# Recurrent attention in a two-layer kernel: another order of the same operations on four engines

## The reference

```python
Fcum = jnp.cumsum(logfg, axis=-1)
Dmat = Fcum[..., :, None] - Fcum[..., None, :] + i_pre[..., None, :]
Dmat = jnp.where(causal, Dmat, -jnp.inf)
m = jnp.max(Dmat, axis=-1, keepdims=True)
Smat = jnp.exp(Dmat - m)
qk = jnp.einsum('bhsd,bhtd->bhst', q, k) / jnp.sqrt(jnp.float32(dqk))
C = qk * Smat
n = jnp.maximum(jnp.abs(jnp.sum(C, axis=-1, keepdims=True)), jnp.exp(-m))
h = jnp.einsum('bhst,bhtd->bhsd', C / n, v)
...
h_out = jax.nn.sigmoid(o_pre) * h_norm
x1 = x + h_out @ w_out
```

## Time and profile before

| | us |
|---|---|
| median of 3 runs (lowest, highest) | 697.85 (697.79, 698.93) |
| the profiled execution's own time | 698.43 |
| its span in the trace | 696.5 |
| PE busy, share of the span | 669.8, 96% |
| DVE | 517.4, 74% |
| ACT | 372.0, 53% |
| POOL | 131.1, 19% |

### The profile page before, as it was taken

The page is one execution under the profiler, slowest core; times in us unless marked ns, Lnnn a source line. Parts: engine busy times, 40 slices in busy tenths (PEclk is TensorE's granted clock), DMA queues, the critical chain, the costliest instruction groups (busy, mean ns, idle before and its releaser), DMA issues.

```text
span 696.5 us, 12153 instructions
## 1 busy us (share of the span) xinstructions
PE 669.8 (96%) x4808; PEld 560.3 (80%) x4808; DVE 517.4 (74%) x919; ACT 372.0 (53%) x775; POOL 131.1 (19%) x125
## 2 busy tenths in 40 slices
PE   7998998999999999999999999999999999999996
PEld 7866775778787888878888878887777898889886
DVE  6736778887956576566675575757679998989996
ACT  5886878846644444344353442446666455364541
POOL 7144535410000020000200002000123213203220
PEclk9999999999999999999999999999999999999999
DMA  5099452000101001010001100150000000000000
GB/s 196 5 264 299 105 155 71 2 1 0 63 1 31 0 1 63 0 31 1 1 23 40 32 1 0 42 233 2 0 1 0 1 2 31 1 31 1 1 31 31
DMA packets 24008, 31.27 MB, mean 45 GB/s; under 512 B 1232, under 2 KB 19952, under 8 KB 23184
## 3 DMA queue, kind: packets, MB, share of 16 engines
q1 hardware_dynamic: 23296, 29.18, 13.6%
q10 hardware_dynamic: 656, 1.31, 0.5%
HBM read 28.18 MB, written 2.31 MB: 44 GB/s over the span
## 4 chain that ended last, share of the span: by engine, by line
PE 66%; DVE 23%; ACT 6%; issue 3%; POOL 1%; DMA 1%; DVEq 0%
PE bank L94 21%; PE bank L96 19%; PE bank L95 19%; DVE l_ring_lo L2544 3%; DVE l_ge L2525 2%; DVE l_h L2540 2%; DVE l_o L2548 1%; DVE h_raw L1220 1%; DVE l_h L2497 1%; ACT m_W L709 1%; PE bank L519 1%; DVE h_ring_lo L1225 1%; DVE m_st L938 1%; PE bank L507 1%; PE bank L492 1%
## 5 line engine op out<-in xcount | busy, mean ns | idle before, releaser
L1220 DVE TENSOR_TENSOR h_raw<-h_s,bank 128x512 f32<-128x512 f32 x104 | 71.4, 686 | 107.9 <-ACT h_s L1210 93.5
L1210 ACT ACTIVATE h_s<-bank 128x512 f32<-128x512 f32 x104 | 62.2, 598 | 164.1 <-PE bank L96 164.0
L1225 DVE TENSOR_TENSOR h_ring_lo<-h_raw,h_ring_hi 128x512 fp32r<-128x512 f32 x92 | 68.9, 749 | 0.1
L1214 ACT ACTIVATE h_ring_hi<-h_raw 128x512 fp32r<-128x512 f32 x104 | 64.7, 622 | 2.3 <-DVE h_raw L1220 2.3
L95 PE MATMUL bank<-fused_lo,h_ring_hi 128*128 128x256 f32 x208 | 58.4, 281 | 0.0
L2244 ACT ACTIVATE l_s<-bank 128x512 f32<-128x512 f32 x32 | 19.1, 598 | 62.7 <-PE bank L96 62.5
L94 PE MATMUL bank<-l_xT_hi,l_wgu 128*128 128x512 f32 x128 | 51.2, 400 | 0.3
L94 PE MATMUL bank<-f_yT_hi,mlp_hi 128*128 128x512 f32 x128 | 50.6, 396 | 0.2 <-DVE f_yT_lo L1333 0.2
L96 PE MATMUL bank<-l_xT_hi,l_lo 128*128 128x512 f32 x128 | 50.0, 391 | 0.0
L95 PE MATMUL bank<-l_xT_lo,l_wgu 128*128 128x512 f32 x128 | 50.0, 390 | 0.0
L96 PE MATMUL bank<-f_yT_hi,fused_lo 128*128 128x512 f32 x128 | 50.0, 390 | 0.0
(11 more groups left out here) (372 smaller groups left out, 1972.8 us busy)
## 6 DMA issues: line engine op xcount, KB each, us to landing
m_W<-m_scratch SPq DMA_DIRECT2D x16, 512.0 KB, 6.8
fused_raw<-in_fused SPq DMA_DIRECT2D x1, 3584.0 KB, 12.9
res<-in_x SPq DMA_DIRECT2D x4, 512.0 KB, 6.1
fused_raw<-in_fused SPq DMA_DIRECT2D x2, 1024.0 KB, 9.3
f_mask<-expert_weights SPq DMA_DIRECT2D x8, 256.0 KB
l_raw<-in_layer SPq DMA_DIRECT2D x1, 2048.0 KB, 8.7
out_x<-res SPq DMA_DIRECT2D x16, 128.0 KB, 1.9
f_xw<-in_turned_x SPq DMA_DIRECT2D x3, 512.0 KB, 5.5
```

The source lines that it names most:

```text
L1210: self.nc.scalar.activation(self.s[u % 2][r, :], gate[r, :], ACT.Silu).then_inc(self.silu.sem, 1)
L1214: self.nc.scalar.activation(self.unit(i, u)[0], self.product(i, u), ACT.Copy).then_inc(self.hi.sem, 1)
L1220: self.nc.vector.tensor_tensor(out=self.product(i, u), in0=self.s[u % 2][r, :], in1=up[r, :], op=ALU.mult).then_inc(self.hidden.sem, 1)
L1225: self.nc.vector.tensor_tensor(out=lo, in0=self.product(i, u), in1=f32(hi), op=ALU.subtract).then_inc(self.lo.sem, 1)
```

## The change

The same instructions are issued, in another order on PE, ACT, DVE and POOL; SP's list is the same. The helper `gated_sum` is dissolved into `sum_squares` and `gate`. On PE, in a batch, `score` and `weighted` come earlier against the projections and `local_state`. On ACT `weights(n+4)` comes before the tanh, `high_h` before `copy_values`, `evict(b, 3)` before `weights(n+5)`; at the end two splits come before the last evictions and the silu before `normal_x`. On DVE `normal_x` moves from the end of a batch to between `sum_squares` and `gate`, ahead of the batch's third `weigh_scores`; `weigh_q` goes behind `weigh_scores`. On POOL `after_norm(b-1, 1)` goes from ahead of the masks to behind the last one.

```diff
@@ tensor, start @@
-        following.hid.credit_down(pe)
...
         idle_products(6)
+        following.hid.credit_down(pe)
@@ tensor, batches @@
+            score(n + 1)
             if b:
                 project_k(b + 1)
+            if b:
                 project_q(b + 1)
-            score(n + 1)
             turn_k(b + 1)
+            weighted(b, 0)
+            score(n + 2)
             local_state(b, 0)
-            weighted(b, 0)
             project_v(b + 1, 0)
             if b:
                 turn_h(b - 1, 1)
-            score(n + 2)
             local_state(b, 1)
             weighted(b, 1)
             project_v(b + 1, 1)
+            score(n + 3)
             if b:
                 project_out(b - 1, 1)
             output_gate(b + 1, 0)
-            score(n + 3)
+            weighted(b, 2)
             local_state(b, 2)
-            weighted(b, 2)
             output_gate(b + 1, 1)
             turn_h(b, 0)
+            weighted(b, 3)
             score(n + 4)
-            weighted(b, 3)
             project_out(b, 0)
         b, n = B - 1, N - C
+        weighted(b, 0)
         score(n + 1)
         local_state(b, 0)
-        weighted(b, 0)
         score(n + 2)
         local_state(b, 1)
         weighted(b, 1)
         score(n + 3)
-        local_state(b, 2)
         turn_h(b - 1, 1)
         weighted(b, 2)
+        local_state(b, 2)
@@ scalar, start @@
         copy_k(0)
+        copy_values(0, 0)
         act.wait_ge(const_ready, CONSTANTS)
         copy_q(0)
-        copy_values(0, 0)
         copy_values(0, 1)
-        copy_keys(0)
         act.wait_ge(rows_t, 1)
         nc.scalar.activation(x_rows[0:B * C, 0, :], rows_banks[0], ACT.Copy)
+        copy_keys(0)
...
+        decay_of_queries(0)
         act.wait_ge(dve_tables, DEC)
         nc.scalar.activation(dexp[:, :, :], dec[:, :, :], ACT.Exp).then_inc(act_tables, 1)
-        decay_of_queries(0)
...
         weights(0)
-        decay_of_queries(3)
         copy_k(1)
         weights(1)
+        decay_of_queries(3)
@@ scalar, batches @@
             evict(b, 0)
-            copy_values(b + 1, 0)
             if b:
                 high_h(b - 1, 1)
+            copy_values(b + 1, 0)
             weights(n + 3)
             evict(b, 1)
             copy_values(b + 1, 1)
+            weights(n + 4)
             output_gate(b + 1, 0)
-            weights(n + 4)
             evict(b, 2)
             output_gate(b + 1, 1)
             high_h(b, 0)
+            evict(b, 3)
             weights(n + 5)
-            evict(b, 3)
@@ scalar, end @@
         following.squares(act)
         high_h(b - 1, 1)
+        following.split_high(act, 0, 2)
         evict(b, 2)
         following.scale_y(act)
-        following.split_high(act, 0, 2)
         following.high_y(act)
         evict(b, 3)
         high_h(b, 0)
+        following.silu(act, 0)
         normal_x(b)
-        following.silu(act, 0)
         high_h(b, 1)
         high_h(b, 2)
+        following.hid.act_hi(act, 0, 0)
         following.split_high(act, 2, following.OPEN)
-        following.hid.act_hi(act, 0, 0)
@@ gpsimd, batches @@
                 inverse_root(b - 1, 1)
-                after_norm(b - 1, 1)
             mask_weights(n + 4)
...
             mask_weights(n + 7)
+            if b:
+                after_norm(b - 1, 1)
@@ vector, start @@
-        following.hid.credit_hidden(dve)
...
         low_y(0)
+        following.hid.credit_hidden(dve)
...
+        weigh_scores(0)
         dve.wait_ge(act_tables, EA_K)
         weigh_q(0)
-        weigh_scores(0)
@@ vector, batches @@
                 mean_square(b - 1, 1)
+            if b:
+                sum_squares(b - 1, 1)
+            if b:
                 add(b - 1, 0)
-                gated_sum(b - 1, 1)
+            if b:
+                gate(b - 1, 1)
+            weigh_scores(n + 1)
             weigh_q(b + 1)
-            weigh_scores(n + 1)
...
             mean_square(b, 0)
+            sum_squares(b, 0)
+            normal_x(b)
+            gate(b, 0)
             if b:
                 add(b - 1, 1)
-            gated_sum(b, 0)
...
             weigh_scores(n + 4)
-            normal_x(b)
@@ vector, last batch @@
         mean_square(b - 1, 1)
+        sum_squares(b - 1, 1)
         add(b - 1, 0)
         weigh_scores(n + 1)
         carry(b, 0)
-        gated_sum(b - 1, 1)
+        gate(b - 1, 1)
...
         mean_square(b, 1)
-        gated_sum(b, 1)
+        gate(b, 1)
         following.split_low(dve, 0, 1)
+        sum_squares(b, 1)
         norm(b, 0)
         following.low_y(dve)
         mean_square(b, 2)
-        gated_sum(b, 2)
+        sum_squares(b, 2)
         low_h(b, 0)
+        add(b - 1, 1)
+        gate(b, 2)
+        following.split_low(dve, 1, 2)
         norm(b, 1)
-        add(b - 1, 1)
         norm(b, 2)
-        following.split_low(dve, 1, 2)
         following.hidden(dve, 0)
         low_h(b, 1)
+        add(b, 0)
         low_h(b, 2)
-        add(b, 0)
         following.split_low(dve, 2, following.OPEN)
         add(b, 1)
+        following.split_low(dve, following.OPEN, following.known["mlp_down"])
         add(b, 2)
         following.hid.dve_lo(dve, 0, 0)
-        following.split_low(dve, following.OPEN, following.known["mlp_down"])
```

More of the change, by code:

```diff
@@ L1000, in mean_square @@
             nc.vector.tensor_reduce(out=den[f][3][:, x], in_=sq[:, some, :].rearrange("p c (h d) -> p (c h) d", d=DV), op=ALU.add, axis=AX.X).then_inc(ms_steps.sem, 1)
-        def gated_sum(b, f):
-            sum_squares(b, f)
-            gate(b, f)
         def sum_squares(b, f):
```

## The result

The changed kernel takes 693.09 us (median of 4 runs, 692.77 to 694.83) against 698.16 for the kernel before beside it: ratio 0.9928, 95% interval 0.9914 to 0.9942, so 5.1 us or 0.7% faster. Predicted were 694.0, that is 3.9 us faster. The profiled execution took 692.77 us with a span of 690.9 (before 698.43 and 696.5).

A forecast was written before the change was run, and what follows sets the result against it. TensorE, busy 96% of the span, was taken as the bound, with 9.35 us removable in stalls and slow clock. Batches 2.5, tail 1.3 and last steps 0.1 gave 3.9 us off the median 697.85: 694.0, range 692.4 to 696.9.

The forecast's parts named there:

- batches: Batches before the tail: stalls of 4.11 us become 1.35; less 0.25 for rounding, a gain of 2.5 us.
- Tail: Last batch's attention: stalls of 3.84 us become 3.4 and the slow clock costs less, gain 0.4 + 0.9 = 1.3 us.
- Stalls before project_q, 1.33 and 0.68: project_q waits for add(b-1,0); with normal_x moved and score(n+1) earlier, 0.68 goes and 0.35 of 1.33 is left.
- score(2) ahead of project_v, score(3) ahead of output_gate: Batch 0: scores move into the stalls of 1.06 and 1.04 us; left about 0.3 and 0.4, plus 0.3 before weighted(0,1).
- No new stall inside a batch: TensorE's waits within a batch: margins thin, smallest 0.25 us, counted 0; bound 0.3 us at three places in two batches.
- The masks: GpSimd: masks start earlier without gain; norm may meet them and end 0.4 or 1.5 us late; counted 0.
- The slow clock costs some 0.5 instead of 1.4: Tail: project_out(2,1) at low clock fits into the time before turn_y, which gives 0.9 us of the gain.
- what is late next is ACT: 15 us in a row: Tail, from evict(2,3): ACT's chain of weights, evictions, squares, high_h, splits and scale_y leaves TensorE waits of 1.9 and 0.9 us.
- The low level left as soon as TensorE was busy again.: Argument against a slower result by the clock in the tail, based on the low clock in the earlier profile.
- The tail gives nothing: Rival: ACT's 15 us chain bounds the tail, only the batches gain 2.5 us, 695.35; chance 0.12.
- Slower: the clock: Rival: low clock holds from the tail's idle 1.9 and 0.9 us through gates(1), costing 9 us, 703; chance 0.04.
- Everything fits better: Rival: a third of the stalls left in tail and batches goes and the clock stays high, 2.1 us more, 691.85; chance 0.08.

The follow-up runs named there:

- e2: Kernel before with only the last batch in the new order on all engines, start and loop old: 696.19 us, ratio 0.9959.
- e1: Kernel before with only the loop over batches 0 to 2 in the new order on all four engines: 694.88 us, ratio 0.994.
- e7: Kernel before plus 9 unused 128x128 identity products on TensorE in the last batch's stall of 1.93 us: 698.04 us, ratio 0.9992.
- e4: Changed kernel with normal_x back at the end of the batch on VectorE, behind the fourth weigh_scores: 697.76 us, ratio 0.9985 to the kernel before.
- e11: Kernel before with one edit, normal_x(b) on VectorE moved between sum_squares(b,0) and gate(b,0): 696.48 us, ratio 0.9973.
- e5: Changed kernel with TensorE's old order in the loop; ACT, VectorE and GpSimd keep the new one: 693.81 us.
- e3: Changed kernel with GpSimd's wait after_norm(b-1,1) back ahead of the two masks: 694.66 us.
- e8: Changed kernel with the two weight splits on ACT back behind scale_y: 692.91 us.
- e10: Kernel of e9 plus 7 unused identity products on TensorE ahead of output_gate(0,0), near 30.5 us: 696.68 us.
- e9: Changed kernel with the last batch in another new order (high_h before squares, weighted(3,3) before turn_y, gates before the last project_outs): 695.95 us.
- e12: The changed kernel measured again without any edit, on the chip of e9 to e11: 693.64 us, ratio 0.9931 to the kernel before.

## Why the prediction was right, point by point

- **The sum, 3.9 us.** Measured 5.1 by the medians, 4.5 at equal clock. The terms, from the table: batches 2.5 predicted; measured 0.4 before project_out(0,0) (62.18 in e2, which has the old code and full clock there, against 61.80) and 1.9 in the loop, together 2.3. That these agree is partly luck. The prediction's own figures give 1.1 for batch 0 (1.06 + 1.04 less 0.3 + 0.3 + 0.4) and 1.7 for the two stalls of the loop, before the 0.25 that it takes off; batch 0 gave 0.4 and the loop 1.9. In batch 0 it left out the stall before score(1), 1.08 in e2, which the profile of before hides behind a low clock and which the new order does not remove. Tail 1.3 predicted, 2.3 measured (19.47 to 17.14). Last steps 0.1 predicted, 0.5 measured (566.9 to 566.4); 0.4 of it is the wait for h_ring_lo behind the span's 142 us, 0.71 instead of 1.08 (e1 and e7, with the old tail, have 1.08 and 1.07).
- **Stalls before project_q, 1.33 and 0.68.** Right: predicted 0.35 and none, measured 0.27 and none. The figure of 1.33 itself varies in the old order, 1.33, 1.23 and 0.73 in before, e2 and e7; in the seven other profiles with all the new lists of the loop the wait is under 0.15. That normal_x is the main cause is shown by e4 and e11; that score(n+1) ahead of project_k has a part is shown by e5, where the first stall is 0.83.
- **score(2) ahead of project_v, score(3) ahead of output_gate.** They happen as worked out (score(2) at 46.82, predicted 46.6), and the stalls left at 50.47 and 54.33 are 0.41 and 0.37. But their worth was over-rated: e5 loses 0.2 to 0.7 us in all without them, since the waiting moved to 44.01 and 45.96.
- **No new stall inside a batch.** Right, but for one of 0.15 us before project_v(3,1), one of the two places named as thinnest (0.25 us).
- **The masks.** The step was right: norm is 0.4 to 0.8 us longer, and off TensorE's path, since with norm back at 0.68 (e3) the second batch of the loop takes 22.49 us for 22.51. The Trainium skill's rule (SBUF — State Buffer, Who interferes with whom) agrees with norm at 69.47 and 91.98 and with L1002 at 63.08, 1.12 us instead of 0.19. It does not hold for the pow, which also reads SBUF: L1025 at 119.15 took 0.68 us beside it.
- **The tail: the term that was mis-sized.** "The slow clock costs some 0.5 instead of 1.4" counted time that was no loss: e7 takes the slow clock away and gains 0.4, because ACT and VectorE set the end. And "what is late next is ACT: 15 us in a row" (its terms add up to 14.5) named one of two bounds; by e8 it is VectorE's list that holds gates(0). The stalls came out near: 0.6, 1.9 and 0.9 predicted, 0.70, 1.63 and 0.71 measured. The gain came from where I saw it, sum_squares early (the pow starts 2.7 us after project_out(2,0), before 5.7) and normal_x away from score(14). By single profiles, the 2.3 us are 0.4 that go with the clock (before to e7), 1.4 of the tail's own lists (e7, 19.08, to e2, 17.68), and 0.5 of the loop's order on top (e2 to changed). The prediction had the tail's own stalls at 0.4 and the clock at 0.9.
- **"The low level left as soon as TensorE was busy again."** A misreading of the earlier trace rows: TensorE was busy for all 3.80 us in which the clock was 0.57. The low level began within 0.3 us of its taking up work again and held for 3.8 us.
- **The signs.** The pow came at 110.07 ("near 112") and gates(2) started at 133.36 instead of 138.41 ("near 134.5"), both somewhat earlier, as the whole was.
- **The rivals.** "The tail gives nothing" is excluded by e2. "Slower: the clock" did not come in any profile with all the new lists, but it is not unreal: in e10 the clock was low over gates(0), and the rest took 1.6 us longer than in e9, not 9. "Everything fits better" is half true, by the tail.

Partly open: why one line that gives 1.6 us when added alone (e11) costs 3.9 when taken away alone (e4). The two moves do not stand in the same surroundings. In e11 VectorE ends up waiting 0.86 us for ACT's evict(2,3), and the tail gets only 0.3 us up to local_state(3,2) (9.8 us after project_out(2,0), before 10.1), where e1 gets 1.0. In e4 the new lists add to what stands before score(14): weigh_scores(13) starts 4.2 us after weigh_scores(12), in the kernel before 3.7 and in the changed one 2.9, because the three steps of sum_squares (0.5 us) now stand ahead of it as well as normal_x (1.3). The stall is 2.00 us and not 1.21 because weighted(3,0), 0.7 us, no longer stands between the two scores to fill it. What the low clock from 117.4 to 120.7 us in e4 adds, I did not separate.

## What to carry to other kernels

In a kernel whose engines run lists written by hand, look for an operation that nobody waits for soon (here normal_x, 1.3 us) standing ahead of one that somebody waits for (the add, the next weigh_scores), and put it where its engine waits anyway; this one line was the largest of the parts that were tested alone. A stall on TensorE is not the price of what stands before it: e7 and e8 removed 1.4 and 0.7 us of slowness or stall and got 0.4 and nothing, since the next chain was right behind. And before you move work away from a gap (e9), ask what filled it and where it will have to be done instead. When a figure differs between profiles, look first at how much it differs between profiles of the same lists: a whole loop varied by 1.8 us here, its second batch by 0.03.

## What the runs showed of the hardware that was not expected

- The granted clock falls to one half near 40 us of the span in some profiles of a kernel and not in others, for some 3.3 us (e7) to 9.7 us (e4). For the changed kernel it is 1.00 from 38 to 40 us in one profile and 0.53 in the other (e12), and the two executions took 692.77 and 692.78 us; 7 more products near 31 us did not prevent it. Low stretches also stand from 11 to 19 us, near 120 us and in the last 2 us of the span. The spread of 697.25 to 701.05 us for one kernel goes with the mean clock over the whole run; how much of it is the stretch near 40 us was not separated.
- Behind a stall of 1.78 to 2.00 us in the tail the clock was low for 3.3 to 7 us in before, e4, e10 and e11, and was not in e9 (1.79 us).
- TensorE sometimes stands for 0.2 to 1.1 us between two products of one group with no wait that the trace shows. The places repeat: before the last 14 of the 64 products of weighted(0,3) in e1, e3, e8, e9 and e12 (0.65, 0.98, 0.20, 0.64 and 0.65 us), and before the last 2 of the 8 products of a score in e3 and e9 (1.12 and 0.84 us), 126 products later. No profile of the kernels with TensorE's old loop shows one of 0.15 us or more. The cause is open.
- A pow on GpSimd over 128x16 elements (2.90 us) leaves VectorE's instructions with two SBUF inputs at their usual time, while an affine_select over 128x1024 (1.09 us) holds them up until its end (L1002 at 63.08: 1.12 us instead of 0.19).
